# Moving low parts of weights from VectorE to GpSimd in a two-FFN, one-attention kernel

## The reference

```python
x = x + 0.5 * ffn(layernorm(x), w_gate, w_up, w_down)
x = x + attention(layernorm(x), Wq, bq, Wk, bk, Wv, bv, Wo, bo)
x = x + 0.5 * ffn(layernorm(x), w_gate, w_up, w_down)

def ffn(x, w_gate, w_up, w_down):
    h = silu(x @ w_gate) * (x @ w_up)      # 256 -> 1024
    h = keep_2_largest_of_4(h)             # by magnitude, in groups of four
    return h @ w_down                      # 1024 -> 256
```

## Time and profile before

| | us |
|---|---|
| median of 3 runs | 767.45 (767.24 to 767.81) |
| the profiled execution, its own time | 766.51 |
| its span in the profile | 764.8 |

### The profile page before, as it was taken

One profiled execution on the slowest core, in us unless ns is written; L12 is line 12 of the kernel. 1 busy time (PEld: TensorE's weight loads), 2 busy tenths in 40 slices (PEclk: granted clock), 3 DMA queues, 4 the chain that ended last, 5 costly groups with the idle time before them and its releaser, 6 DMA issues.

```text
span 764.8 us, 15941 instructions
## 1 busy us (share of the span) xinstructions
PE 731.7 (96%) x5322; PEld 518.2 (68%) x5322; DVE 683.9 (89%) x1985; ACT 510.3 (67%) x1022; POOL 260.7 (34%) x362
## 2 busy tenths in 40 slices
PE   5999999989999999999999999999999999999997
PEld 4787888887776555555555555555555587888886
DVE  5989999987699999999999999999985679989897
ACT  5644443324426899999999999999999734443441
POOL 2143435018642222333222233255335203434330
PEclk9999999999999999999999999999999999999999
DMA  8100000007773213433223433524322000000001
GB/s 319 58 1 1 0 1 1 1 6 257 209 223 73 60 39 69 96 80 71 50 47 80 88 77 99 126 54 88 81 67 50 14 8 1 1 27 1 28 2 55
DMA packets 28017, 49.90 MB, mean 65 GB/s; under 512 B 4896, under 2 KB 13248, under 8 KB 27424
## 3 DMA queue, kind: packets, MB, share of 16 engines
q1 hardware_dynamic: 27936, 48.90, 24.6%
HBM read 20.35 MB, written 14.88 MB: 46 GB/s over the span
## 4 chain that ended last, share of the span: by engine, by line
PE 67%; DVE 21%; issue 5%; POOL 4%; ACT 3%; DMA 1%; PEldq 0%; PEld 0%; DVEq 0%; POOLq 0%; ACTq 0%
PE att_o_ps L1586 18%; PE att_s_ps L1570 12%; PE att_m_ps L1529 11%; PE ffn_gate L218 7%; PE ffn_up L218 6%; PE ffn_y_ps L364 5%; DVE ffn_hs L557 2%; DVE ffn_h L599 2%; DVE att_maxima L1662 2%; DVE ffn_xn L181 2%; PE out_y_ps L1250 2%; DVE att_scratch L1659 2%; POOL qkv_turned L913 1%; DVE ffn_rank L543 1%; DVE ffn_pair_min L532 1%
## 5 line engine op out<-in xcount | busy, mean ns | idle before, releaser
L1712 ACT ACTIVATE att_probs<-att_s_ps 128x512 f32<-128x512 f32 x626 | 304.5, 573 | 20.0 <-PE att_s_ps L1570 17.3
L1659 DVE CUSTOM_DVE_ANT_0 att_scratch<-att_m_ps,att_causal 128x384 bf16<-128x384 f32 (+3 forms) x512 | 221.4, 486 | 10.1 <-PE att_m_ps L1529 9.3
L1529 PE MATMUL att_m_ps<-k,q 64*128 64x256 f32 (+3 forms) x768 | 205.5, 362 | 6.1 <-DVE att_maxima L1659 2.7
L1570 PE MATMUL att_s_ps<-q,k 64*128 64x512 f32 (+2 forms) x750 | 201.6, 378 | 0.9 <-ACT att_probs L1712 0.3
L1570 PEld LDWEIGHTS att_s_ps<-q,k 64*128 64x128 f32 x750 | 116.3, 184 | 65.9 <-ACT att_probs L1712 53.3
L1586 PE MATMUL att_o_ps<-att_probs,att_vs 128*32 128x512 f32 (+3 forms) x1536 | 156.4, 496 | 0.1
L1529 PEld LDWEIGHTS att_m_ps<-k,q 64*128 64x128 f32 x768 | 120.1, 184 | 52.4 <-DVE att_maxima L1659 24.2
L1764 POOL TENSOR_SCALAR_AFFINE_SELECT att_probs<-att_probs 128x512 f32<-128x512 f32 x128 | 79.6, 639 | 117.9 <-ACT att_probs L1712 117.7
L663 POOL TENSOR_TENSOR ffn_hs_lo<-ffn_hs,ffn_hs_hi 128x512 fp32r<-128x512 f32 x48 | 77.4, 1636 | 107.2 <-ACT ffn_hs_hi L459 107.2
L488 ACT ACTIVATE ffn_a<-ffn_h 128x512 f32<-128x512 f32 x64 | 40.4, 632 | 106.7 <-DVE ffn_h L599 106.7
L1662 DVE TENSOR_REDUCE att_maxima<-att_m_ps 128x1 f32<-128x512 f32 x128 | 86.7, 687 | 7.3 <-PE att_m_ps L1529 5.7
(11 more groups left out here) (146 smaller groups left out, 1351.4 us busy)
## 6 DMA issues: line engine op xcount, KB each, us to landing
q_rows<-qkv_parts SPq DMA_DIRECT2D x16, 512.0 KB, 4.6
q<-q_rows SPq DMA_DIRECT2D x32, 256.0 KB, 4.4
q<-q SPq DMA_DIRECT2D x16, 512.0 KB, 4.3
k<-k_rows SPq DMA_DIRECT2D x16, 160.0 KB, 5.4
k_rows<-qkv_parts SPq DMA_DIRECT2D x8, 256.0 KB, 3.3
k<-k SPq DMA_DIRECT2D x16, 128.0 KB, 4.6
out_num<-att_sums SPq DMA_DIRECT2D x128, 16.0 KB
x<-in_x SPq DMA_DIRECT2D x1, 1536.0 KB, 11.4
```

The costliest lines, as they stand in the source:

```text
L1529: pe.matmul(m_ps[unit_bank(n)][:, COLUMNS[m]], q[g % 2][m_lane, t // TPC, h, t % TPC * P:(t % TPC + 1) * P], k[g % 2][m_lane, keys], start ...
L1570: last = pe.matmul(s_all[S_BANK["s", n]][:, at:at + w], k[g % 2][lane, kb * P:(kb + 1) * P], q[g % 2][lane, qc, h, q0:q0 + w], start=True, ...
L1659: dve.tensor_tensor_reduce(out=scratch[bank][:, at], in0=m_ps[bank][:, at], in1=causal[:, N - n:], scale=1.0, scalar=LOWEST, op0=ALU.add, ...
L1712: act.activation(probs[u % len(probs)][:, h, SPAN[u]], s_all[S_BANK["s", n]][:, SPAN[u]], ACT.Exp, scale=SCALE).then_inc(exp_done, 1)
```

## The change

Four edits, all in the first FFN:

1. `first_low_parts` (gate 0, GpSimd) now also waits until all four tiles of chunk 0 are normalised.
2. The low parts of the two down weights move from VectorE to GpSimd (`down_low_parts`): the first after the reciprocal deviation of chunk 1, the second when chunk 1 is normalised.
3. The low part of the projection's weights moves from VectorE to GpSimd, behind the four `hs_lo` of the first block.
4. The waits for 6 low parts become waits for 4 of VectorE and 2 of GpSimd.

```diff
-    def first_low_parts(self, pool):
+    def first_low_parts(self, pool, normed):
         _, _, read, hi, lo = self.loads[0]
+        pool.wait_ge(normed.xn_ready, normed.TPC)
         pool.wait_ge(self.hi_ready, 1)
         for k in range(read.shape[1]):
             pool.tensor_tensor(lo[:, k], read[:, k], hi[:, k].bitcast(F32), ALU.subtract).then_inc(self.gate_lo_ready, 1)
+
+    def down_low_parts(self, pool, blk):
+        _, _, read, hi, lo = self.loads[4 + blk]
+        pool.wait_ge(self.hi_ready, 4 + blk + 1)
+        pool.tensor_tensor(lo, read, hi.bitcast(F32), ALU.subtract).then_inc(self.down_lo_ready, 1)
...
         if first_loads:
-            pe.wait_ge(w_loads.ready, 6)
+            pe.wait_ge(w_loads.down_lo_ready, BLKS)
...
         if follower:
-            act.wait_ge(w_loads.ready, len(w_loads.loads))
+            act.wait_ge(w_loads.ready, 2 * BLKS)
+            act.wait_ge(w_loads.down_lo_ready, BLKS)
             follower.high_weights(act)
...
-        stage(0, 0, sparse=False, add=False, extra={0: 2, 1: 3, 2: 4, 3: 5} if first_loads else {})
+        stage(0, 0, sparse=False, add=False, extra={0: 2, 1: 3} if first_loads else {})
         stage(0, 1, add=False)
-        if follower:
-            follower.low_weights(dve)
...
             if first_loads:
-                w_loads.first_low_parts(pool)
+                w_loads.first_low_parts(pool, normed)
         normed.inverse_deviation(pool, 1)
+        if first_loads:
+            w_loads.down_low_parts(pool, 0)
+            pool.wait_ge(normed.xn_ready, 2 * TPC)
+            w_loads.down_low_parts(pool, 1)
         low_parts(0, 0)
+        if follower:
+            follower.low_weights(pool)
```

More of the change, by code:

```diff
@@ L236, in __init__ @@
         self.gate_lo_ready = ctx.enter_context(nc.semaphore(f"{tag}_w_gate_lo_ready"))
+        self.down_lo_ready = ctx.enter_context(nc.semaphore(f"{tag}_w_down_lo_ready"))
     def high_parts(self, act, n):
@@ L700, in sync @@
         if follower:
-            sp.wait_ge(w_loads.ready, len(w_loads.loads))
+            sp.wait_ge(w_loads.ready, 2 * BLKS)
+            sp.wait_ge(w_loads.down_lo_ready, BLKS)
     return Programs(tensor, scalar, vector, gpsimd, sync)
@@ L827, in high_weights, with low_weights @@
         act.activation(w_hi[:], w_raw, ACT.Copy).then_inc(w_hi_ready, 1)
-    def low_weights(dve):
-        dve.wait_ge(w_hi_ready, 1)
-        dve.tensor_tensor(w_lo[:], w_raw, w_hi[:].bitcast(F32), ALU.subtract).then_inc(w_lo_ready, 1)
+    def low_weights(pool):
+        pool.wait_ge(w_hi_ready, 1)
+        pool.tensor_tensor(w_lo[:], w_raw, w_hi[:].bitcast(F32), ALU.subtract).then_inc(w_lo_ready, 1)
     FILLS = {(e, UNITS - 1): [(e, h) for h in range(group_rows.QPK)] for e in range(2)}
```

## The result

| | before | changed |
|---|---|---|
| median of 17 runs each, us | 768.2 | 770.89 |
| lowest and highest, us | 766.35, 773.55 | 768.76, 773.68 |
| ratio, with 95% interval | | 1.0028 [1.0017, 1.004] |
| profiled execution, own time, us | 766.51 | 770.89 |
| its span, us | 764.8 | 769.2 |

The changed kernel is 2.7 us slower by the medians; forecast was 2.8. The ratio is not that of the medians: 1.0028 of 768.2 is 2.2 us, and its interval 1.3 to 3.1 us.

The account below looks back on a forecast made before the run. VectorE and TensorE were both taken as tight in the first 55 us, with GpSimd's subtractions locking VectorE out. -0.8 + 1.8 + 1.8 = +2.8 us on the 767.45 median makes 770.2 us; range 766.8 to 772.2.

Parts of the forecast that it names:

- Step 1: Wait before gate 0: xn run undisturbed, TensorE's product with the second half comes at 13.8, h0 to h3 0.8 us earlier.
- Step 2: Down weights on GpSimd: xn, then pair_max wait for its subtractions; +1.8 us, together +1.0 at h5 to h7.
- hand-over: Between GpSimd and VectorE: some 0.2 us of two alternating instructions overlaps, read from hs and hs_lo.
- the saved 1.14 us: In front of h4: VectorE's gain from losing the second wd_lo, spent on xn waiting for GpSimd; h4 at 28.05.
- The bound for the slow rate: Down weights: with GpSimd's 1024 columns at 3.14 us, the total at this point is +1.9 us.
- rival C: Much slower: long GpSimd subtractions take 3.14 and 5.10 us; +5.1, to 772.5 us; chance 0.07.
- Step 3: Projection's weights on GpSimd: pair_max or pair_min waits for qkv_w_lo, h9 at 51.9; +1.8 us, together +2.8.
- Nothing absorbed it behind h9: From h9 to chunk 2's transposes VectorE has no pause, so everything there comes 2.8 us later.
- A: Faster: GpSimd's long subtractions don't hold VectorE up for their length; 3.3 us gained, to 764.1; chance 0.12.
- B: No change: one of the collisions, down weights' or projection's, stays out; 767.6 or 767.2 us; chance 0.15.
- the rate of gate 0: GpSimd's subtraction for gate 0, read in steps: 1.57 us for 512 columns, giving 3.14 for 1024 and 5.10 for 1664.
- the sum from the rows: GpSimd's 1664 columns priced from the trace's contiguous subtractions at 2.2 ns a column: 1.30 + 2.57 = 3.87 us.

Follow-up runs that it names:

- Edit 1 by itself: Kernel before, with only GpSimd's gate 0 low parts waiting for chunk 0's four xn: 766.27 us against 768.3; again on another chip, 766.51 against 768.26.
- the down weights alone: Kernel before, with only the two down weights' low parts moved from VectorE to GpSimd: 769.89 us against 768.3, ratio 1.0015.
- the repeat: The changed kernel, nothing altered, run again on another chip against the kernel before: 771.28 us against 768.26, ratio 1.0032.
- the trace without falls: Profiles of the repeat and of the changed kernel with 14 unused transposes in TensorE's pause; the latter took 771.38 us against 767.78.
- the pieces: Changed kernel, with each GpSimd wd_lo cut into four subtractions and qkv_w_lo into eight: 768.63 us against 768.3 for the kernel before, ratio 0.9997.
- the two parts alone: Kernel before, with only the down weights' low parts on GpSimd (769.89 us), or only the projection's (770.37 us), each against 768.3.
- fills of 1.49: Three GpSimd memsets of 1664 columns added to a version with edit 1, down 1 moved on VectorE and qkv_w_lo halved on GpSimd: 767.15 us, 766.27 without.

## Why the prediction was right

Each step against what the profile of the changed kernel shows:

| step | predicted | measured |
|---|---|---|
| 1: h0 | -0.8 | -0.81 |
| 2: h5, together | +1.0 | +0.73 |
| step 2 by itself | +1.8 | +1.52 |
| 3: h9, together | +2.8 | +2.64 |
| step 3 by itself | +1.8 | +1.91 |
| GpSimd, 1024 columns | 2.44 | 2.41, 2.39 |
| GpSimd, 1664 columns | 3.87 | some 3.8 |
| medians | +2.8 | +2.7 |

**Step 1** was right in its order and size: three subtractions in turns, and a product at 13.70 where 13.8 was worked out. Edit 1 by itself is a gain, shown twice.

**Step 2** was right in its mechanism and 0.3 us too large. h4 came at 27.69 instead of the 28.05 that was worked out. GpSimd's `wd_lo` ended at 26.65, and the first `xn` was to begin its work then; but the second `xn` stands at 26.72, one start-to-start of 0.32 behind, so the first began at 26.4. I had counted the hand-over of some 0.2 at `pair_max` and left it out at `xn`. That the saved 1.14 us of the second `wd_lo` is spent on waiting for the first one was the least plain claim, and the down weights alone show it (h4 minus h3 2.73 against 3.04). The bound for the slow rate was worked out twice, as +1.9 in step 2 and as 1.0 + 0.7 + 0.4 = +2.1 under rival C; the forecast doesn't use either.

**Step 3** was right: the silu behind `qkv_w_hi` held h8 at 45.06, the two engines took turns as `hs_lo`, `pair_max`, `qkv_w_lo`, `pair_min`, in this order, and 2 us of work less on VectorE became 1.9 us more of time.

**Nothing absorbed it behind h9:** h12 was at 67.13 (64.51 before), +2.62. The statement on TensorE was not complete. I wrote that it runs without pauses worth naming from there; the pause for `hs_lo` grew from 1.44 to 1.81 us, and the clock fell behind it in the profiled execution. The transposes of chunk 2 came 4.2 us later than before in that execution, not 2.8; in the repeat without that fall they were 2.4 us behind before. That the median held all the same fits that executions of the kernel before lose clock in places as well, so that this does not add to the difference in full; it was not shown.

**The number** is closer than the steps earn. They miss by -0.3 and +0.1 us, the trace without falls gives 2.4 to 2.7, and the interval is 1.3 to 3.1 us. The mechanism is what is confirmed; the agreement of the medians to 0.1 us is luck in part.

**The rivals.** A (not held) is refuted by `pair_max` at 3.03 and `pair_min` at 4.80 us, and by the pieces. B (one collision absent) is refuted by the same two rows, one for each collision; the two parts alone each show theirs too. C (the slow rate) is refuted by 2.41 and some 3.8 us: the rate of gate 0, 1.53 for 512 columns here, does not come with the length.

The estimate that the prediction worked out from the Trainium skill ("GPSIMD Engine Reference", "Elementwise — side-by-side cycle accounting") was 3.65 us for the 1664 columns; the runs show some 3.8, nearer to the sum from the rows.

By the Trainium skill, "SBUF — State Buffer", section "Who interferes with whom", a GpSimd instruction that only writes SBUF does not contend with VectorE's two-input instructions. The trace agrees: 1.21 and 0.68 us beside fills of 1.49.

## What to carry to other kernels

Before work goes from VectorE to GpSimd, look at what VectorE does beside it: if it reads two SBUF tensors or normalises, the time of the moved instruction can be added to VectorE's, and as GpSimd takes about twice as long (2.40 against 1.22 us here for 1024 columns), the move costs more than it saves. Put it beside VectorE instructions that have an input in PSUM, or cut it into pieces of the length of a wait that can be afforded, which made the loss smaller here but left 1.0 us of it; where an order has to hold, a wait on the other engine's result can be a gain, as edit 1 is. An idle stretch of one of the two may be what the other is working in, so filling it is not free either.

## What the runs showed of the hardware

- GpSimd's subtraction of two contiguous operands took 0.63 us for 208 columns, 1.30 for 512 and 2.40 for 1024, and some 2.0 and 3.8 us for 832 and 1664, where its wait inside has to be taken off: about 2.2 ns a column and 0.16 us, up to 1664 columns.
- The wait is inside the instruction: `pair_min` of 1.21 us shows as 4.80, with no idle time in front of it. On either engine it looks like work.
- Two instructions that exclude each other alternate one by one when both engines have a queue: pieces of 0.63 us then took 1.61 beside VectorE's 1.21, which took 1.65.
- TensorE's clock fell to 1.2 GHz for stretches of 3 to 4 us in places that differ from execution to execution of the same kernel (62 to 66 us in one, 38 to 44 in another, 172 to 176 or 174 to 180 in both). Every profile here, that of the kernel before too, has one more between 744 and 762. Behind pauses of 1.81 and 1.84 us it fell once and once did not. The stretch at 62 us cost 1.5 us at once, of which 1.0 was left a chunk later.
